# Starting the attention items of a latent-attention stage before the row maxima of the second unit are taken

## The reference

```python
q = (x @ Wq.T).reshape(b, t, 16, 16)...          # 16 heads of 16
latent = layernorm(x @ Wdkv.T, ln_g, ln_b)       # 128 wide
k, v = latent @ Wuk.T, latent @ Wuv.T
q, k = apply_rope(q), apply_rope(k)
scores = where(causal, q k^T / sqrt(16), -inf)
attn = softmax(scores); out = attn @ v @ Wo.T
```

## Time and profile before

| | |
|---|---|
| median of 3 executions | 2920.75 us (2916.05 to 2923.26) |
| the profiled execution | 2923.26 us, its span 2921.5 us |
| PE busy | 2698.3 us, 92% of the span |
| DVE busy | 1424.7 us, 49% |
| ACT busy | 1099.7 us, 38% |
| latent attention of the first batch, first chunk to last product | 451.3 to 643.9 us |
| the same, other batches | from 1101.3, 1749.9 and 2403.8 us |

### The profile page before, as it was taken

One profiled execution on the slowest core, in us unless ns is written; L12 is line 12 of the kernel. 1 busy time (PEld: TensorE's weight loads), 2 busy tenths in 40 slices (PEclk: granted clock), 3 DMA queues, 4 the chain that ended last, 5 costly groups with the idle time before them and its releaser, 6 DMA issues.

```text
span 2921.5 us, 39584 instructions
## 1 busy us (share of the span) xinstructions
PE 2698.3 (92%) x14422; PEld 1619.2 (55%) x14423; DVE 1424.7 (49%) x3994; ACT 1099.7 (38%) x2108; POOL 312.4 (11%) x521
## 2 busy tenths in 40 slices
PE   7999988999999988989999988999999989996998
PEld 4565654345556554345556554345556554356997
DVE  3434466644333466644343566643443566643443
ACT  3444232443443323444543423444442423441221
POOL 1000010022000010022000010122000010113111
PEclk9999997999999998999999998989999997998999
DMA  3000000001000000001000000001000000022111
GB/s 95 11 12 1 15 1 1 1 13 40 12 12 1 15 1 1 1 13 40 17 6 1 15 1 1 1 13 46 12 6 1 15 1 1 1 123 86 54 54 40
DMA packets 32411, 56.84 MB, mean 19 GB/s; under 512 B 6980, under 2 KB 23442, under 8 KB 31858
## 3 DMA queue, kind: packets, MB, share of 16 engines
q1 hardware_dynamic: 27490, 41.56, 4.6%
q0 software_dynamic: 4752, 13.02, 1.2%
HBM read 40.24 MB, written 14.32 MB: 19 GB/s over the span
## 4 chain that ended last, share of the span: by engine, by line
PE 82%; DVE 8%; issue 4%; ACT 4%; POOL 2%; DMA 0%; SPq 0%; DVEq 0%; ACTq 0%; POOLq 0%
PE ps L939 9%; PE ps L1146 9%; PE ps L911 8%; PE ps L884 8%; PE ps L1177 6%; PE ps L1191 5%; PE ps L869 5%; PE ps L929 5%; PE ps L1259 4%; PE ps L1273 4%; PE ps L894 4%; PE ps L1031 3%; PE ps L1049 2%; PE ps L840 1%; PE ps L1060 1%
## 5 line engine op out<-in xcount | busy, mean ns | idle before, releaser
L1146 PE MATMUL ps<-arena 32*128 32x512 f32 (+3 forms) x1536 | 468.0, 582 | 38.5 <-DVE arena L1528 28.6
L778 ACT ACTIVATE arena<-ps 128x1024 f32<-128x1024 f32 (+3 forms) x384 | 301.8, 811 | 451.7 <-PE ps L1177 449.8
L1361 DVE TENSOR_REDUCE neg_max<-ps 128x1 f32<-128x128 f32 (+7 forms) x256 | 194.0, 758 | 568.0 <-PE ps L914 567.7
L1177 PE MATMUL ps<-arena 32*128 32x512 f32 (+3 forms) x1536 | 321.1, 540 | 2.4 <-ACT arena L778 2.4
L939 PE MATMUL ps<-arena 128*128 128x512 f32 (+3 forms) x768 | 318.1, 501 | 4.8 <-ACT arena L691 0.7
L691 ACT ACTIVATE arena<-ps 128x512 f32<-128x512 f32 (+3 forms) x384 | 188.7, 492 | 294.6 <-PE ps L929 292.6
L911 PE MATMUL ps<-arena 128*128 128x512 f32 (+3 forms) x768 | 290.7, 489 | 4.5 <-ACT arena L700 4.5
L1146 PEld LDWEIGHTS ps<-arena 32*128 32x128 f32 x1536 | 195.7, 206 | 177.6 <-DVE arena L1528 90.0
L884 PE MATMUL ps<-turned_t,arena 128*128 128x512 f32 x512 | 229.5, 602 | 1.1 <-ACT turned_t L662 1.1
L1177 PEld LDWEIGHTS ps<-arena 32*128 32x128 f32 x1536 | 139.6, 194 | 146.1 <-ACT arena L778 75.4
L1523 DVE TENSOR_REDUCE arena<-ps 128x1 f32<-128x512 f32 x256 | 165.7, 686 | 107.1 <-PE ps L1146 106.3
(11 more groups left out here) (211 smaller groups left out, 3766.7 us busy)
## 6 DMA issues: line engine op xcount, KB each, us to landing
arena<-in_w_qkv SPq DMA_DIRECT2D x32, 384.0 KB, 3.1
arena<-in_w SPq DMA_DIRECT2D x2, 4096.0 KB, 17.6
xin<-in_x SPq DMA_DIRECT2D x5, 1024.0 KB, 5.4
xres_ids<-sorted_res SPq DMA_DIRECT2D x35, 129.0 KB, 2.2
xin<-sorted_rows SPq DMA_DIRECT2D x35, 128.0 KB, 2.0
w_out<-in_w_out SPq DMA_DIRECT2D x1, 1024.0 KB
out<-xin,out_row POOLq DMA_INDIRECT x35, 2.9
sorted_res<-xin SPq DMA_DIRECT2D x4, 129.0 KB, 2.5
```

Of the source, the lines that this page charges most:

```text
L778: nc.scalar.activation(mprobs_t[n % BUFS][:, 2 * pair:2 * pair + 2, lo:BANK], ps[:, bank:bank + 2, 0:BANK - lo], ACT.Exp).then_inc(mexp_do ...
L1146: nc.tensor.matmul(ps[:, MAX_BANK[m], 0:n], q_heads_t[rows_j, g, t * P:(t + 1) * P], k_heads_t[rows_j, g, c * BANK:c * BANK + n], start=Tr ...
L1177: last = nc.tensor.matmul(ps[:, 3 + j, 0:hi - lo], k_heads_t[rows_j, g, kb * P:(kb + 1) * P], q_heads_t[rows_j, g, lo:hi], start=True, sto ...
L1361: nc.vector.tensor_reduce(neg_max[:, par, t:t + 1], ps[:, buf:buf + 2, :].rearrange("p a n -> p (a n)")[:, 0:n], AX.X, ALU.max, negate=Tru ...
```

## The change

Items begin when the first unit's maxima are in place, not the first two units'. PE issues 22 chunks alone (16 and the lead of 6). Then the chunks of the unit after the one whose items run are spread evenly over its blocks: 2 a block in the first unit (16 chunks over 8 blocks), 4 a block in the second (32 over 8), 2 a block in the three that follow (32 over 16), 1 a block in the sixth (16 over 16), 2 a block in the seventh until chunk 192, none in the eighth. Unit by unit: 22 alone, then 16, 32, 32, 32, 32, 16, 10, 0. Seven banks serve only the first 16 chunks; from m = 16 chunks have three. The wait for all of the first two units before item 0 goes. The last `turn_max` is issued just ahead of item 44, the first of the last unit, where it was ahead of item 39.

```diff
-ALONE = FIRST_CHUNK[2]
...
-        bank = m % 7 if m < ALONE else m % 3
+        bank = m % 7 if m < FIRST_CHUNK[1] else m % 3
...
 def chunks_by(n, block):
 
-    return min(ALONE + LEAD + 2 * (2 * n + block + 1), CHUNKS)
+    u = unit_of(FIRST_ITEM, n)
+    if u + 1 == len(UNITS):
+        return CHUNKS
+    i, more = n - FIRST_ITEM[u], FIRST_CHUNK[u + 2] - FIRST_CHUNK[u + 1]
+    blocks = 2 * (FIRST_ITEM[u + 1] - FIRST_ITEM[u])
+    return min(FIRST_CHUNK[u + 1] + LEAD + more * (2 * i + block + 1) // blocks, CHUNKS)
...
-                issued = ALONE + LEAD
+                issued = FIRST_CHUNK[1] + LEAD
                 chunks(0, issued)
                 pe.wait_ge(kt_taken, b * (2 * NG) + 2 * NG)
-                pe.wait_ge(ms_taken, b * MAX_SLOTS + chunk_count(ALONE - 1, TAKE_LEAD) + 1)
                 for n in range(ITEMS):
-                    if issued == CHUNKS and chunks_by(n - 2, 1) < CHUNKS:
+                    if n == FIRST_ITEM[-2]:
                         turn_max(len(UNITS) - 1)
```

## The result

The changed kernel takes 2991.88 us (median of 4, 2977.59 to 2994.81) against 2922.01 us for the kernel before, measured beside it (median of 4, 2916.05 to 2928.28). The ratio is 1.0236, with an interval of 1.0206 to 1.0266: slower, and 42 us above the end of my range. The forecast of 2925 us was wrong. The profiled execution took 2979.47 us with a span of 2977.7 us, 56.2 us more than before. It is one of the shorter ones: the medians lie 69.9 us apart, and its mean granted clock was 0.939, against 0.932 in the two executions of 2994.7 and 2994.8 us. What follows explains the 56.2 us; the other 14 us have no trace.

The account below looks back on a forecast made before the run. The prediction saw three regimes: chunks alone at a low clock, a first unit slowed by the clock, then units limited by three banks. About +1 us a batch, +4 us in four, gave 2925 us; range 2900 to 2950 us.

Parts of the forecast that it names:

- Chunks alone: Stretch of each batch before item 0: 11.6 us in the first batch, 12.6 us saved, about 12.2 us in shorter-stage batches.
- First unit: First 4 items of a batch, with 16 chunks: 17.0 + 0.4 + 1.0 = 18.4 us, 1.4 us lost.
- rival of the early clock: Items starting 12 us sooner restore the clock in the first unit: 3 us less a batch, 2913 us at most; chance 0.15.
- Second unit: Four items with 32 chunks on three banks, summed as a chain: 28.2 us against 14.9, 13.3 us lost a batch.
- PEclk be 1.00: Sign for the second unit: PE's granted clock is full there; the prediction is wrong if it is under 1.00.
- the clock falls in the second unit: Slower rival: PE waits for banks and drops to half clock, 12 us a batch, 2973 us, or 2949 if midway; chance 0.13.
- items 8 to 31: Middle piece of a batch, where both kernels have gone equally far in chunks: costed at nothing.
- no gap there is over 1.5 us, and products, which brought it back, run in each item: Argument against a clock fall in the second unit, a fall priced at 12 us a batch.
- Third unit: Unit after the crowded one, within the piece costed at no change: 30.0 us in the first batch.
- Fourth and fifth: Units within the piece costed at no change: 30.0 and 28.2 us in the first batch.
- Last three: Units from item 32 on: 47.3 us together, 48.3 before; -1.0 us a batch, bounds -3 and +1.
- the saving ahead and the loss behind nearly cancel: Per batch: -12.6 + 1.4 + 13.3 = +2.1 us (or +1.5) up to item 8, then -1.0, about +1 us.

Follow-up runs that it names:

- the run with 64 columns: The changed kernel, but DVE takes the maximum over only the first 64 keys of each chunk issued in the second unit; 2918.28 us in one run, before 2927.09 us.

## Why the prediction was wrong

*Chunks alone: right.* 11.6 us predicted, 11.6, 11.6, 11.6 and 11.4 measured. In the first batch the 12.6 us were saved, in the others 11.4 to 12.8.

*First unit: wrong, by the clock.* I let the clock return 3.2 us after the first product, from the earlier trace rows. It returned at 465.4, 3.7 us after the first score and 4.4 us before any product (469.75), and the unit took 14.0 us in place of 18.4. In the third batch it never returned (20.4 us, PE busy for 20.33). My rival of the early clock (0.15) held here three times in four, 11.6 us in all, and was small beside the rest.

*Second unit: the step that failed.* The sum of 28.2 us was made at the full clock: "PEclk be 1.00" was among what would show it. It was 0.58, 0.58, 0.54 and 0.67. The sum's other readings came true: DVE busy for 19.57 us (19 said), PE before its chunks for DVE in the middle of the blocks. What happened is the rival "the clock falls in the second unit", which I priced at 12 us a batch and gave 0.13; my range ended at half of its price. Against the sum the units were 9.4 to 15.4 us longer, mean 12.7, and the clock alone cost 13.8 us in the run with 64 columns. Another 2.6 us went in the third unit, in items 8 to 31, which I had put at nothing: the clock that has fallen doesn't return at the unit's border. The argument against it, "no gap there is over 1.5 us, and products, which brought it back, run in each item", took two things for a protection that they weren't: the clock fell after 3.30 us without a gap worth the name, and in the first batch the products of each item ran at half speed for 24 us before it came back, for 3.4 us.

Was the evidence there? Yes: the earlier trace rows have 9.9 us of PE busy at 0.50, the state that the second unit then had for 35 of its 41.7 us. I read them as a delay before the return and should have read them as a state in which this kind of work can stay. The Trainium skill (TensorE: Matmul & The Clock Gate, part 1, the HAM clock gate) says that the throttled clock is the default and that sustained matmul activity lifts it. In this trace PE's busy time alone didn't lift it: busy for 20.33 of 20.40 us at 0.50 in the third batch. The same part of the Trainium skill warns that how long a kernel runs cold differs from run to run. The trace agrees within one execution: first units of 14.0, 15.6 and 20.4 us for the same instructions. It puts the penalty of this ramp, the time at the low clock when matmuls start, under 1% of a typical kernel span. The loss here, 2.4%, is more than such a ramp, for the clock fell in the middle of the work.

*Third unit:* predicted 30.0, measured 32.5, 32.8, 32.5, 32.5, from the clock's late return. *Fourth and fifth:* 29.9 and 28.3 us, for 30.0 and 28.2 predicted. *Last three:* 47.5 us (608.3 to 655.8) for the 47.3 predicted in the first batch, and this was in part luck: at the full clock the new order takes 46.0 us, and a dip of the clock in the eighth unit, which I hadn't foreseen, made up the difference.

*Without the clock?* Whether the change would then be faster no run shows. It saves 12.6 us alone, and 3 us of the first unit if the clock comes early as it did here, so it gains as long as the crowded unit takes less than 14.9 + 15.6 = 30.5 us. That unit at the full clock lies between 24.5 and 34.2 us, on either side of it. In the run with 64 columns, which has no waits for DVE there, the three batches that held the clock took 188.6, 192.6 and 188.6 us, against 191.2, 195.2 and 192.6 before, and the one that lost it 205.0 against 192.6. The 2918 us of that run say nothing on this: its four batches sum to 3.2 us more than those in the trace of before, so what made it shorter lay outside this stage. So the forecast that the saving ahead and the loss behind nearly cancel was neither borne out nor refuted: the clock hid it.

*What tips the clock* is shown only in part. The waits for DVE: without them three of four units hold it to their end, and with DVE's work doubled an ordinary unit runs at 0.89 in place of 1.00. The state at the start: the longest second units follow first units at 0.50. The kind of work: fillers on all rows raise it from 0.58 to 0.71 and once to 1.00. Each of the three moved it and none decides it: a unit without the waits fell (38.3 us), and three that began at 1.00 fell. Nor does the number of chunks an item: first units with 4 an item stayed at 0.50 to their end (20.4 us, and 19.4 us in the order of before), and a sixth unit with 2 an item fell to 0.76, though the units of the earlier trace rows ran at 1.00 from the second on. Crowding made a low clock likelier here; all eight crowded units of the changed kernel had one. What decides it, and why two batches of one execution differ, stays open.

## What to carry to other kernels

Before work is moved so that a stretch gets denser in matmuls on part of the rows, read the granted clock over the nearest stretch of the same mix in the trace, and price the new stretch at that clock as well; if it has ever stayed at 0.50 with PE busy, treat this as the likely case and not as a rival. An overlap that crowds a few buffers wins little: 12.6 us saved ahead cost 24.5 - 14.9 = 9.6 us behind even where no reader made PE wait and the clock held. A run that takes out the reader's time (64 columns in place of up to 512) separates the waits from the clock.

## What the runs showed of the hardware

- The granted clock can stay at 1.2 GHz with PE busy almost without a break: 20.33 of 20.40 us in the third batch, 25.13 of 25.30 us with three chunks a block.
- The instructions alone don't fix it: second units of 38.3 and 24.5 us, second units of 34.2 and 41.4 us, each pair from one kernel and one execution.
- Once down it can outlast the work that went with it: back at 523.4, 6 us after the crowded unit had ended. And it can return for 3.4 us in the middle of such work and fall again (502.9 to 506.3).
- A few matmuls on all rows need not cost anything although they add work: with five of about 1.1 us a batch, in a stretch that they didn't shorten, the kernel was 0.3% faster (0.9968, 0.9945 to 0.9992), and the two units behind them ran at 0.96 where the earlier trace rows show 0.79.
